# Keys with the four window columns innermost, the normalised row worked out on GpSimd, and the loops written out

## What is computed

```python
part = x.reshape(n, H // w0, w0, W // w1, w1, c)
part = part.transpose(0, 1, 3, 2, 4, 5).reshape(n * NW, WS, c)
qkv = (part @ qkv_w.T + qkv_b).reshape(n * NW, WS, 3, N_HEAD, HEAD_DIM)
q, k, v = (qkv[:, :, 0] * SCALE, qkv[:, :, 1], qkv[:, :, 2])
attn = jnp.einsum('wihd,wjhd->whij', q, k)
attn = attn.reshape(n, NW, N_HEAD, WS, WS) + bias[None, None] + MASK[None, :, None]
attn = jax.nn.softmax(attn, axis=-1).reshape(n * NW, N_HEAD, WS, WS)
out = jnp.einsum('whij,wjhd->wihd', attn, v).reshape(n * NW, WS, c)
...
h = jnp.einsum('tbld,hd->tblh', x, W) + b
return lif_multistep(h)
...
x = x + _L0_conv_ref(_gn(x), L0_conv_qkv_w, L0_conv_qkv_b, L0_conv_bias_table)
x = x + _L1_conv_ref(_gn(x), L1_conv_W, L1_conv_b)
```

## Time and profile before

| | |
|---|---|
| median of 3 runs | 545.47 us (545.28, 545.47, 548.49) |
| the profiled execution | 546.64 us |
| its span, first to last instruction | 544.9 us |
| mean granted TensorE clock in it | 0.962 |
| busy: PE, its weight loads, DVE, ACT, POOL | 80%, 74%, 73%, 69%, 51% |
| DMA | 155272 packets, 65.78 MB, of them 124978 under 512 B |

### The profile page before, as it was taken

How to read it: one execution, slowest core, us unless ns; L and a number is a source line. 1 busy time by engine, 2 the same in 40 slices (tenths; PEclk the granted TensorE clock), 3 DMA queues, 4 the chain that set the end, 5 groups by cost and what they waited for, 6 DMA issues and landing times.

```text
span 544.9 us, 20474 instructions
## 1 busy us (share of the span) xinstructions
PE 434.2 (80%) x7912; PEld 403.4 (74%) x7912; DVE 398.2 (73%) x838; ACT 377.4 (69%) x863; POOL 280.3 (51%) x382
## 2 busy tenths in 40 slices
PE   0056658889878986988698879889988887889997
PEld 0056558878868886978698779778888776778886
DVE  5753757777776877677767767778877676588897
ACT  2353657878886887678778867788888786756551
POOL 6163456556654766475647654765685556640000
PEclk9996979999998999899989988999999998899999
...
GB/s 204 67 81 65 140 75 107 142 142 155 138 139 109 141 138 137 109 128 142 138 114 133 139 131 112 129 140 134 123 118 119 111 125 80 2 78 136 135 137 135
DMA packets 155272, 65.78 MB, mean 121 GB/s; under 512 B 124978, under 2 KB 142644, under 8 KB 155188
## 3 DMA queue, kind: packets, MB, share of 16 engines
...
...
## 4 chain that ended last, share of the span: by engine, by line
PE 38%; SPq 21%; ACT 11%; DMA 10%; issue 9%; DVE 8%; ACTq 1%; POOL 0%; DVEq 0%; POOLq 0%
SPq L317 12%; SPq L311 7%; DMA k_stack<-k_spill0lo 4%; PE pv_ps L1050 4%; PE proj_ps L939 3%; DMA k_stack<-k_spill1lo 3%; PE proj_ps L940 3%; PE proj_ps L941 3%; PE score_ps L1026 3%; PE score_ps L1016 3%; PE proj_ps L926 3%; PE pv_ps L926 3%; PE score_ps L926 3%; ACT xn L493 2%; ACT v_hi L529 2%
## 5 line engine op out<-in xcount | busy, mean ns | idle before, releaser
L454 POOL TENSOR_TENSOR p_lo<-probs,p_hi 128x512 f16<-128x512 f32 x128 | 146.4, 1165 | 147.3 <-ACT p_hi L608 122.9
L1016 PE MATMUL score_ps<-q_stack,k_stack 96*128 96x64 f16 x1024 | 88.1, 197 | 50.5 <-ACT max_rows L598 39.2
L1016 PEld LDWEIGHTS score_ps<-q_stack,k_stack 96*128 96x128 f16 x1024 | 74.2, 100 | 56.8 <-ACT max_rows L598 47.7
L785 DVE TENSOR_REDUCE neg_max<-max_ps 128x16 f16<-128x1024 f32 x64 | 78.4, 1225 | 42.9 <-PE max_ps L996 41.3
L607 ACT ACTIVATE probs<-score_ps 128x512 f32<-128x512 f32 x128 | 76.9, 601 | 38.4 <-PE score_ps L1026 37.6
L779 DVE TENSOR_TENSOR v_lo<-proj_ps,v_hi 64x256 f16<-64x256 f32 x128 | 54.2, 423 | 59.3 <-ACT v_hi L529 58.4
L939 PE MATMUL proj_ps<-xn_hi,w_hi 128*128 128x256 f32 x256 | 76.8, 300 | 10.7 <-DVE w_lo L738 7.2
L1012 PE MATMUL score_ps<-both_parts,bias_k 128*128 128x64 f16 x1024 | 80.8, 197 | 0.0
L608 ACT ACTIVATE p_hi<-score_ps 128x512 f16<-128x512 f32 x128 | 77.3, 604 | 0.0
L1012 PEld LDWEIGHTS score_ps<-both_parts,bias_k 128*128 128x128 f16 x1024 | 72.8, 100 | 2.8
L940 PE MATMUL proj_ps<-xn_lo,w_hi 128*128 128x256 f32 x256 | 73.8, 288 | 0.0
...
## 6 DMA issues: line engine op xcount, KB each, us to landing
...
```

Of the source, the lines that this page charges most:

```text
L454: pool.tensor_tensor(p_lo[p][:, quads, :, :].rearrange("p g w i -> p (g w i)"), probs[:, quads, :, :].rearrange("p g w i -> p (g w i)"), p ...
L785: dve.tensor_reduce(neg_max[:, :].rearrange("p (m n) -> p m n", m=2)[:, :, 0:8], max_ps[:, :, :].rearrange("p m (n j) -> p m n j", j=WS), ...
L1016: pe.matmul(dst, k_stack[slot][0:96, 2 * mid + q, at, :], q_stack[slot][0:96, 2 * mid + q, at, :], start=False, stop=False)
```

## The change

It has four parts. The keys lie with the four window columns innermost: ACT and DVE write `k_flat` through the view `keys_of`, and `k_stack` is `[128, QUADS, HALVES, 128, WCOLS]`, so that a run of a stack load is 64 x 4 f16 = 512 bytes; TensorE then reads 128 keys of a window with a step of four f16, as the moving operand of L996 and as the weights of L1016. ACT no longer writes `xn`: it writes `xn_hi` straight from `xc` in two halves, and does so at the start of a p = 1 pair, around `q_high`. POOL works out `xn` itself (two `tensor_scalar` of 128x256) ahead of the subtraction. The `Fori` loops are written out.

```diff
         flags = sb("flags", [128, 2], f32)
-        xn = [sb(f"xn{i}", [128, HALVES * ROWTOK], f32) for i in range(2)]
+        xn = sb("xn", [128, HALVES * ROWTOK], f32)
         xn_hi = [sb(f"xn_hi{i}", [128, HALVES * ROWTOK], f32r) for i in range(2)]
...
         q_stack = [sb(f"q_stack{i}", [128, QUADS, HALVES * WCOLS, WS], f16) for i in range(2)]
-        k_stack = [sb(f"k_stack{i}", [128, QUADS, HALVES * WCOLS, 128], f16) for i in range(2)]
+        k_stack = [sb(f"k_stack{i}", [128, QUADS, HALVES, 128, WCOLS], f16) for i in range(2)]
         q_spill = [[nc.dram_tensor(f"q_spill{i}{part}", [32, QUADS, HALVES * ROWTOK], f16).ap() for part in ("hi", "lo")] for i in range(2)]
...
-            for k in range(BODY):
-                body(k, k // 2, k, 0)
-            with eng.Fori(1, SAMPLES - 2) as s:
-                for k in range(BODY):
-                    body(s * BODY + k, s * WROWS + k // 2, k, s)
-            for s in (SAMPLES - 2, SAMPLES - 1):
+            for s in range(SAMPLES):
                 for k in range(BODY):
...
-            body(0)
-            with eng.Fori(1, WROWS - 1) as y:
+            for y in range(WROWS):
                 body(y)
-            body(WROWS - 1)
...
+        def keys_of(buf, part):
+            if buf is k_flat:
+                return buf[:, part, :].rearrange("p (h j w) -> p h w j", h=HALVES, w=WCOLS)
+            return buf[:, part, :].rearrange("p (h w j) -> p h w j", h=HALVES, w=WCOLS)
...
                     rows = slice(first + e * D, first + (e + 1) * D)
-                    sp.dma_start(k_stack[slot][rows, quads, :, e * WS:(e + 1) * WS],
-                                 k_spill[slot][part][e * D:(e + 1) * D, quads, :].rearrange("d g (n j) -> d (g n) j", j=WS))\
+                    sp.dma_start(k_stack[slot][rows, quads, :, e * WS:(e + 1) * WS, :].rearrange("r g h j w -> r (g h) (j w)"),
+                                 k_spill[slot][part][e * D:(e + 1) * D, quads, :].rearrange("d g (h n) -> d (g h) n", h=HALVES))\
                       .then_inc(stacked[slot], 16)
...
             def clear_stack(slot):
-                return pool.memset(k_stack[slot][:, :, :, :].rearrange("p g n j -> p (g n j)").bitcast(f32), 0.0)
+                return pool.memset(k_stack[slot][:, :, :, :, :].rearrange("p g h c w -> p (g h c w)").bitcast(f32), 0.0)
...
-            def low_part(slot, done):
+            def low_part(slot, row, sample, norm, done):
+                pool.wait_ge(norm_ready, norm)
+                wait(pool, xn_lo_done, done - 1)
+                for h in range(HALVES):
+                    col = bass.ds(sample * HALVES + h, 1)
+                    tok = slice(h * ROWTOK, (h + 1) * ROWTOK)
+                    last = pool.tensor_scalar(xn[:, tok], one(xc, row)[:, tok], rstd[:, col], shift[:, col], ALU.mult, ALU.add)
+                last.then_inc(xn_done, 1)
+                pool.wait_ge(xn_done, done)
                 pool.wait_ge(xn_hi_done, done)
-                pool.tensor_tensor(xn_lo[slot][:, :], xn[slot][:, :], xn_hi[slot][:, :].bitcast(f32), ALU.subtract)\
+                pool.tensor_tensor(xn_lo[slot][:, :], xn[:, :], xn_hi[slot][:, :].bitcast(f32), ALU.subtract)\
                     .then_inc(xn_lo_done, 1)
...
-            low_part(0, 1)
+            low_part(0, 0, 0, 1, 1)
             for buf in v_hi[1:] + v_lo[1:]:
...
             zeroed.then_inc(const_step, 1)
-            low_part(1, 2)
+            low_part(1, 1, 0, 1, 2)
             pool.wait_ge(const_step, 10)
...
                 if p == 0 and not is_last_row(row, 2):
-                    low_part(k // 2 % 2, row + 3)
+                    sample = s + (k // 2 + 2) // WROWS
+                    low_part(k // 2 % 2, row + 2, sample, sample + 1, row + 3)
...
-            def normed(dst, row, sample, norm):
+            def normed(dst, row, sample, norm, halves=range(HALVES)):
...
                 act.wait_ge(norm_ready, norm)
-                for h in range(HALVES):
+                for h in halves:
                     col = bass.ds(sample * HALVES + h, 1)
...
-            def normalise(row, sample, slot, norm, done):
-                wait(act, xn_lo_done, done - 1)
-                normed(xn[slot], row, sample, norm).then_inc(xn_done, 1)
-            def xn_high(slot, done):
-                act.wait_ge(xn_done, done)
-                wait(act, v_ps_done, done - 2)
-                act.activation(xn_hi[slot][:, :], xn[slot][:, :], ACT.Copy).then_inc(xn_hi_done, 1)
+            def xn_high(slot, row, sample, norm, done, halves=range(HALVES)):
+                if 0 in halves:
+                    wait(act, v_ps_done, done - 2)
+                last = normed(xn_hi[slot], row, sample, norm, halves)
+                if HALVES - 1 in halves:
+                    last.then_inc(xn_hi_done, 1)
...
                 wait(act, k_hi_spilled, 16 * (done - 1))
-                act.activation(k_flat[:, 0, :], proj_ps[:, 1, :], ACT.Copy).then_inc(k_hi_done, 1)
+                act.activation(keys_of(k_flat, 0), keys_of(proj_ps, 1), ACT.Copy).then_inc(k_hi_done, 1)
...
             act.activation(b_rows[:, :], b_raw, ACT.Copy).then_inc(setup_act, 1)
-            normalise(0, 0, 0, 1, 0)
-            xn_high(0, 1)
-            normalise(1, 0, 1, 1, 1)
+            xn_high(0, 0, 0, 1, 1)
             act.wait_ge(setup_dve, 3)
...
             v_high(0, 1, 1)
-            xn_high(1, 2)
+            xn_high(1, 1, 0, 1, 2)
             bias_high(0)
...
                 if is_first(n, 1):
-                    normalise(2, 0, 0, 1, 2)
+                    xn_high(0, 2, 0, 1, 3)
                     q_high(2)
                     k_high(2)
-                if p == 0 and not is_last_row(row, 2):
-                    xn_high(k // 2 % 2, row + 3)
-                if p == 1 and not is_last_row(row, 2):
-                    q_high(row + 3)
-                    k_high(row + 3)
+                if p == 1:
+                    sample = s + (k // 2 + 3) // WROWS
+                    for h in range(HALVES):
+                        if not is_last_row(row, 3):
+                            xn_high(nxt % 2, row + 3, sample, sample + 1, row + 4, (h,))
+                        if not is_last_row(row, 2):
+                            (q_high, k_high)[h](row + 3)
                 if v_now:
...
                     v_high(1, 2, 1)
-                if p == 1 and not is_last_row(row, 3):
-                    sample = s + (k // 2 + 3) // WROWS
-                    normalise(row + 3, sample, nxt % 2, sample + 1, row + 3)
                 if is_first(n, 2):
...
                 wait(dve, k_lo_spilled, 16 * (done - 1))
-                dve.tensor_tensor(k_flat[:, 1, :], proj_ps[:, 1, :], k_flat[:, 0, :], ALU.subtract).then_inc(k_lo_done, 1)
+                dve.tensor_tensor(keys_of(k_flat, 1), keys_of(proj_ps, 1), keys_of(k_flat, 0), ALU.subtract).then_inc(k_lo_done, 1)
...
                                 last = pe.matmul(max_ps[queries, mid, col:col + 128], q_stack[slot][rows, 2 * mid + q, at, :],
-                                                 k_stack[slot][rows, 2 * mid + q, at, :],
+                                                 k_stack[slot][rows, 2 * mid + q, h, :, 2 * (k % 2) + w],
                                                  start=False, stop=(w == 1 and h == 1))
...
                                     before_tiles()
-                                pe.matmul(dst, k_stack[slot][0:96, 2 * mid + q, at, :], q_stack[slot][0:96, 2 * mid + q, at, :],
+                                pe.matmul(dst, k_stack[slot][0:96, 2 * mid + q, h, :, 2 * p + w], q_stack[slot][0:96, 2 * mid + q, at, :],
                                           start=False, stop=False)
```

## The result

The changed kernel takes 570.65 us (median of 4 runs, 569.71 to 574.14); the kernel before, run beside it, 546.98 (545.28 to 554.74). The ratio is 1.0434, with a 95% interval of 1.0356 to 1.0512: 4.3% slower. The forecast was 552.0 in a range of 539 to 565. The side was right, the size was not: 17 us of the 23.1 us that the profiled execution is longer (569.71 against 546.64) were not in the sum.

What follows compares the result with a forecast made beforehand. GpSimd works nearly without a gap in a plain row (slack 1.77 us), while TensorE waits for ScalarE's `max_rows`. +9.3 + 0.6 - 3.8 = +6.1 us on 546.64 gives 552.7, median 551.6, stated as 552.0; range 539.0 to 565.0.

Steps and rivals of the forecast that it cites:

- The norm wait: ScalarE's `xn_hi` waits for GpSimd's `shift` before `q_flat`, seven times near 5 us; chain +5.08 us in samples 1 to 6.
- The clock: TensorE's clock falls to half behind each norm stall, costing 1.3 us each, with bounds of 0 and 2.6.
- GpSimd's `xn`: GpSimd's two new `tensor_scalar` ahead of the subtraction: 1.0 us together, so `xn_lo` ends 5.49 us after `p_lo` starts.
- t: Time of one GpSimd `tensor_scalar` of 128x256, taken as 0.50 us, between 0.43 and 0.73.
- The keys with a step of 8 bytes: TensorE's strided key reads and the strided writes of `k_flat` cost 0; far bound 100 us for weight loads.
- the terms of the row: Plain row, projection to projection: 4.10 + 2.16 + 4.39 + 2 x 0.50 + 0.2 = 11.85 us, against 12.42 before.
- Rival (C): TensorE or the writers pay for the key step: 560 us at 8 ns per TensorE read, 650 at most; chance 0.15.
- Loops and late loads: Written-out loops remove four jumps, their low clock and late loads; written-out code costs nothing; plain rows count no load wait.
- the 8 x 0.2 of SP's time: On SP, longer k runs make eight load issues cheaper, saving at most 1.6 us.
- the 0.8 of the forecast: Longer k runs make the landing of the key loads perhaps 0.8 us sooner.
- 2.4 us sooner as forecast: At the kernel's start, cheaper issues and sooner landing shorten the 10.4 us load wait by 2.4 us.
- The three stretches: The forecast's parts by sample: samples 1 to 6 +9.3 us, sample 0 with the start +0.6, sample 7 -3.8.

Runs made afterwards that it cites:

- e1: Changed kernel, but in the pair k = 3 both halves of `xn_hi` are written at the pair's end, behind the exponentials: 534.10 us, ratio to before 0.9704.
- e5: e3 with ScalarE and VectorE writing `k_flat` without a step and reading PSUM with a step instead: 528.60 us, ratio to before 0.9670.
- e2: Kernel before, with the sample loop and the spiking layer's loop over y written out, nothing else: 539.55 us, ratio to before 0.9822.
- e10: Changed kernel with `k_flat` written without a step on both engines, PSUM read with the step, norm wait kept: 553.76 us, ratio to before 1.0095.
- e3: Kernel before with loops written out and the changed kernel's key layout, work of ScalarE and GpSimd as before: 548.72 us, ratio to before 1.0035.
- e4: Changed kernel with the key layout of before; loops written out and the new split of ScalarE's work stay: 564.41 us, ratio to before 1.0266.
- e8: Changed kernel with late `xn_hi` as in e1 and `k_flat` written without a step as in e5: 522.50 us, ratio to before 0.9579.
- e9: e8 with GpSimd's two `xn` instructions one pair earlier, in front of `p_lo` of the p = 1 pair: 524.39 us, ratio to before 0.9545.
- e6: e4 with `xn_hi` of the pair k = 3 written at the end of its pair, as in e1: 538.11 us, ratio to before 0.9856.
- e12: e9 with SP's wait for the scores moved behind the spill of the low k part: 523.08 us, ratio to before 0.9503.

## Why the forecast had the side and missed the size

**The norm wait: right.** Forecast: seven waits that cost 5.08 us each on the path and 1.3 of low clock. Measured: seven waits, 5.3 us each, and e1 shows 5.2 to 5.7 apiece in the time, low clock and all, below the forecast's 6.4. By the terms: P to `max_rows` in the norm row is 142.17 - 133.12 = 9.05 us against 4.42 in a plain one, 4.6 more, and the norm rows of samples 1 to 6 take 17.94 on average against 16.93 + 1.3 = 18.23 forecast.

**The clock: right in kind, uneven in size.** Windows of the kernel after, behind the norm stalls of samples 2 and 4 (columns as in the earlier trace rows):

```profile
197.00:200.30 3.30, 2.86 (x64) 2.56 (x65) 2.43 (x2) 2.31 (x6) 0.70 (x1) 0.50 0.34 114
200.30:203.70 3.40, 3.29 (x65) 3.08 (x66) 2.68 (x8) 2.17 (x7) 3.35 (x5) 1.00 0.52 150
```

```profile
308.80:312.20 3.40, 3.40 (x34) 3.40 (x32) 3.06 (x6) 1.77 (x5) 3.10 (x4) 0.50 0.64 192
```

After a stall the granted clock is 0.50, that is 1.2 GHz, for 3.4 us in four of the six samples and for 6.8 in two. With 3.4 the norm row is 17.53 to 17.59, with 6.8 it is 18.37 and 18.98. A plain row and 4.6 of waiting would be 16.86, so by this estimate the low clock costs 0.7, or 1.5 to 2.1; I had 1.3 with bounds of 0 and 2.6. In the second profile of the changed kernel all six stretches are 6.8 long, its clock is low for 82 us in all against 61, and its span is 577.3 against 567.9. That goes some way to explain why two measurements of one kernel differ by 1%.

**GpSimd's `xn`: right.** I took t as 0.50, and two take 1.10; what stands around them took a little less than I gave it. From `p_lo` to the end of `xn_lo` the forecast had 5.49, and it is 132.95 - 127.52 = 5.43.

**The keys with a step of 8 bytes: the step that failed.** The sum put this term at 0, "since the 128 columns and their bytes stay", and ended with "The same sentence holds for the strided writes of `k_flat`". All the weight of the argument lay on TensorE, whose reads did get slower but turned out to be hidden but for 0.1 us a row (3 us in all, e5 against e2). The writers got one sentence, with no place on the path. They are on it: ScalarE's `k_flat` stands right in front of `max_rows`. What the term measured is 18.5 to 22.8 us in the changed kernel (e10) and 20 with the layout alone (e5 against e3). With it at 20 the forecast would have been 572. The other way round, e10, the changed kernel without this price, takes 553.76 against the 552.0 forecast. That it comes so near is in part luck: its undisturbed rows are 0.2 us shorter than forecast, and 7.4 us of late loads, which I had at none, largely make that up. The price sits in the terms of the row: 4.42 in place of 4.10, and 2.33 in place of 2.16, so 12.23 in place of 11.85. With straight writes they are 3.93 and 2.24 and the row is 11.65, 0.2 below the forecast. Rival (C), with a chance of 0.15, named "TensorE or the writers", but its 560 was worked out from TensorE's reads alone, at 8 ns each on the path. They got 65 ns (moving) and 13 ns (weights) slower, nearly off the path. So (C) named the right cause and priced the wrong one.

The Trainium skill, page "SBUF — State Buffer", section "Door 1: The DMA port swizzle", lets two accesses to a 16-byte line run at full rate, by which a step of 8 bytes is free. This kernel's rows contradict it for f16: 597 to 1327 ns on ScalarE, which only writes with the step, 690 to 1312 on VectorE, which also reads with it, and both back with e5. The measurement decides.

**Loops and late loads: half right.** The jumps were worth 8.8 to 9.7 us (e2). That late loads go with the jumps was wrong (e2 has more of them), but the long runs do remove them: 2.9 us left in e5. In the changed kernel 7.6 us of them stay, in rows that I had counted without any. The slow writers aren't their cause: e10, with straight writes, has 7.4. SP's issues of key loads did not fall to near 0.4 us: the median went from 626 ns to 598. What did fall is the time from issue to landing, from 3.5 to 2.7 us at the median for a full load, the 0.8 of the forecast. So the 8 x 0.2 of SP's time was wrong, and that the first `max_rows` came 2.4 us sooner as forecast (50.05 against 52.42) is no proof of its reason, for e2 has it at 49.29 without the layout.

**The three stretches.** Here the trace is set against the forecast's parts. Samples 1 to 6 took 331.43 against 322.7 (+8.7): 18 plain rows at 12.44 on average in place of 11.85 are +10.6, the norm rows -1.8. Of the 0.59 a plain row, 0.38 is the slower undisturbed row, 12.23, and 0.2 rows that were disturbed. Up to the first pair of sample 1 it was 117.89 against 115.8 (+2.1). From the first pair of sample 7 to the end it was 118.6 against 112.5 (+6.1): the 3.0 us wait for a load did go, as forecast, but four pairs took 27.86 in place of 24.90 with slow writers in them, and the spiking layer 1.8 more. The first goes with the slow writers: in e10 the same four pairs take 24.69. The last 1.8 goes with the clock, at 0.50 for 3.4 us while TensorE is busy all the time (columns as in the earlier trace rows):

```profile
504.10:507.50 3.40, 3.40 (x12) 2.78 (x10) 2.75 (x6) 1.09 (x2) 2.69 (x10) 0.50 0.20 77
```

Every trace whose time from the last `max_rows` to the end is 76.5 to 76.8 us has such a stretch of 3.4 us some 11 to 13 us behind it (the changed kernel twice, e1, e3, e4, e5, e8, e9, e10), and every trace without one takes 74.8 to 74.9 (before, e2, e6, e12). e9 has it and e12 hasn't, with one spill moved between them, so it isn't tied to a part of the change.
